# Order of work in a dense step: first normalised tile turned first, q and logits copied first, q's low part subtracted first

## The reference

```python
x = x + xattn(layernorm(x), ctx, Wq, Wkv_expand, Wout)   # 16 heads of 32, 64 keys, causal mask
x = x + ffn(layernorm(x), ...)
# xattn: q = xn @ Wq.T; scores = q k / sqrt(32); softmax; out = attn v; out @ Wout.T
# ffn:   logits = xn @ router_w.T; top 2 of 8 experts by logit, the logit is the weight;
#        y = silu(xn @ wg) * (xn @ wu) @ wd for each chosen expert, plus a shared expert with biases
```

## Time and profile before

| | before |
|---|---|
| median of 3 runs | 870.39 us (866.59 to 870.81) |
| the profiled execution | 872.62 us, of which the span is 870.9 us |
| busy in the span: TensorE matmul, VectorE | 791.0 us (91%), 614.5 us (71%) |
| ScalarE, GpSimd | 439.7 us (50%), 429.2 us (49%) |
| mean granted TensorE clock | 0.979 of full |

### The profile page before, as it was taken

The page is one execution under the profiler, slowest core; times in us unless marked ns, Lnnn a source line. Parts: engine busy times, 40 slices in busy tenths (PEclk is TensorE's granted clock), DMA queues, the critical chain, the costliest instruction groups (busy, mean ns, idle before and its releaser), DMA issues.

```text
span 870.9 us, 22280 instructions
## 1 busy us (share of the span) xinstructions
PE 791.0 (91%) x7516; PEld 545.4 (63%) x7516; DVE 614.5 (71%) x1196; ACT 439.7 (50%) x805; POOL 429.2 (49%) x530
## 2 busy tenths in 40 slices
PE   4478988989898989898999999999999999999994
PEld 1367776777777768687787787545555455455552
DVE  4978886989898989886557877555555555555552
ACT  3375766777777777777533553333333333333331
POOL 1144856565656656654600001255555555656553
PEclk9789998999999999999999999999999999999998
DMA  9324272635353534334575666488989889988892
GB/s 316 107 73 144 98 218 96 203 118 201 101 211 112 193 118 127 111 108 134 189 249 183 196 197 204 105 142 147 157 145 154 147 142 160 145 146 148 144 149 42
DMA packets 102760, 132.39 MB, mean 152 GB/s; under 512 B 54368, under 2 KB 55392, under 8 KB 101280
## 3 DMA queue, kind: packets, MB, share of 16 engines
q1 hardware_dynamic: 86784, 95.74, 37.3%
q0 software_dynamic: 15904, 35.70, 24.2%
HBM read 71.61 MB, written 52.31 MB: 142 GB/s over the span
## 4 chain that ended last, share of the span: by engine, by line
PE 46%; DVE 6%; ACT 4%; DMA 4%; issue 3%; POOL 3%; POOLq 0%; another core or an unknown queue 0%; ACTq 0%; DVEq 0%; SPq 0%
PE psum L1264 34%; PE psum L1312 8%; PE psum L1255 4%; DMA hidT<-xn2T_f 3%; DVE head_max L995 1%; DVE xy L1005 1%; DVE stats L926 1%; ACT probsT L700 1%; POOL rstd L532 1%; POOL kv_store L568 1%; ACT xn2T L700 1%; DVE w_q L1244 0%; PE psum L1364 0%; DVE hid L1219 0%; ACT attnT L700 0%
## 5 line engine op out<-in xcount | busy, mean ns | idle before, releaser
L680 POOL DMA_INDIRECT out<-w_q,tabs x71 | 112.5, 1584 | 109.1 <-DVE w_q L1244 72.9
L670 POOL DMA_INDIRECT x_in<-normed_tokens,tabs x71 | 71.0, 1000 | 137.6 <-DVE tabs L1130 88.2
L1229 DVE SCALAR_TENSOR_TENSOR hid<-psum,tabs,silu_g 128x256 f32<-128x256 f32 x71 | 34.4, 484 | 110.3 <-ACT silu_g L824 110.3
L1264 PE MATMUL psum<-exp_all,hidT 128*128 x426 | 103.4, 379 | 4.7 <-DMA hidT<-xn2T_f 4.7
L824 ACT ACTIVATE silu_g<-psum,tabs 128x256 f32<-128x256 f32 x71 | 33.7, 474 | 145.0 <-PE psum L1264 134.8
L1312 PE MATMUL psum<-xn1T,w_q 128*128 128x128 f16 x1536 | 93.3, 222 | 6.7 <-DVE xn1T L862 6.7
L1264 PE MATMUL psum<-exp_all,probsT 128*128 x420 | 96.4, 379 | 0.0
L1312 PEld LDWEIGHTS psum<-xn1T,w_q 128*128 128x128 f16 x1536 | 88.5, 99 | 7.1 <-DVE xn1T L862 6.9
L1264 PE MATMUL psum<-w_o,attnT 128*128 128x512 f16 x384 | 88.7, 381 | 0.0
L1264 PEld LDWEIGHTS psum<-exp_all,hidT 128*128 128x128 f16 x426 | 41.7, 98 | 55.8 <-issue 7.7
L530 POOL TENSOR_SCALAR rstd<-moments 128x1 f32<-128x1 f32 x64 | 14.3, 223 | 120.2 <-DVE moments L931 112.8
(11 more groups left out here) (199 smaller groups left out, 1730.2 us busy)
## 6 DMA issues: line engine op xcount, KB each, us to landing
x_in<-x SPq DMA_DIRECT2D x64, 256.0 KB, 3.1
exp_all<-experts SPq DMA_DIRECT2D x8, 1536.0 KB, 8.5
out<-xy SPq DMA_DIRECT2D x32, 256.0 KB, 2.1
normed_tokens<-xn SPq DMA_DIRECT2D x32, 256.0 KB, 2.4
normed_turned<-xn2T SPq DMA_DIRECT2D x32, 256.0 KB, 2.0
w_q<-out SPq DMA_DIRECT2D x32, 256.0 KB, 2.9
out<-w_q SPq DMA_DIRECT2D x32, 256.0 KB, 2.6
probsT<-normed_turned SPq DMA_DIRECT2D x16, 256.0 KB, 3.4
```

The lines of the kernel that those rows point to most:

```text
L670: pool.indirect_dma_start(x_in[:, t % 4, :], None, xn_dram, bass.IndirectOffsetOnAxis(gather_at[:, t:t + 1], 0)).then_inc(gathered[t % 4], 16)
L680: pool.indirect_dma_start(out, bass.IndirectOffsetOnAxis(add_at[:, t:t + 1], 0), y[:, t % Y_RING, :], None, bounds_check=TOKENS - 1, oob_i ...
L1229: dve.scalar_tensor_tensor(hid[:, :], psum[:, GU_BANK[m % 2], I:2 * I], up_scale_at[:, tm:tm + 1], silu_g[:, :], ALU.mult, ALU.mult).then_ ...
L1264: last = pe.matmul(dst, lhsT(a, c), rhs(z, c), start=(c == 0 and a == z == 0), stop=(c == n - 1 and a == 1))
```

## The change

Three engines' queues are put in another order inside a dense step. No instruction is added or taken away, and each keeps its waits.

- ScalarE: the normalisation of t5 into `xn2` goes behind the copies of q and of the logits; the `xn1T` copy of t1 goes ahead of the `xn2T` copy of t5.
- VectorE: the expert's magnitudes go behind the joining of the statistics and the low part of q.
- TensorE: the turns of t1 (`xn1`) go ahead of the turns of t5 (`xn2`).

```diff
 # scalar step
-                if live(t5):
-                    act.wait_ge(ln_rstd[1], t5 + 1)
-                    wait(act, xn2_stored[(j + 1) % 2], 16 * (TPB // 2 * b + (j - 5) // 2))
-                    act.activation(xn2[:, (j + 1) % 2, 0:H], x1, ACT.Identity, bias=rstd[:, 1, 2:3],
-                                   scale=rstd[:, 1, 1:2]).then_inc(xn2_ready, 1)
                 if live(t2):
                     act.wait_ge(q_mm, t2 + 1)
                     copy(flat(qT[:, 0, :, :]), bank(5), Q_DOWN, qT_hi)
                 if live(t6):
                     act.wait_ge(router_mm, t6 + 1)
                     copy(logits[:, bass.ds(t6, 1), :], psum[:, 6, 0:E], sc[:, S_R:S_R + 1], logits_ready)
+                if live(t5):
+                    (the same four lines)
...
+                if live(t1):
+                    act.wait_ge(xn1T_mm, t1 + 1)
+                    copy(flat(xn1T[:, 0, :, :]), bank(7), X_UP, xn1T_hi)
                 if live(t5):
                     act.wait_ge(xn2T_mm, t5 + 1)
                     wait(act, xT_stored, 16 * t5)
                     copy(flat(xn2T[:, 0, :, :]), bank(6), X_UP, xn2T_hi)
-                if live(t1):
-                    (the same two lines)
 # vector step
-                if e is not None and j in ((1, 2, 3) if isinstance(b, int) and b == 0 else (0, 2, 3)):
-                    expert_magnitudes(e, max(0, j - 1))
                 if live(tile):
                     join_stats(0, tile)
                 if live(t2):
                     dve.wait_ge(qT_hi, t2 + 1)
                     low(flat(qT[:, 1, :, :]), bank(5), Q_DOWN, flat(qT[:, 0, :, :]), qT_ready)
+                if e is not None and j in (...):
+                    expert_magnitudes(e, max(0, j - 1))
 # tensor step
+                if live(t1):
+                    pe.wait_ge(xn1_ready, t1 + 1)
+                    wait(pe, xn1T_ready, t1)
+                    transposes(bank(7), xn1[:, :], C, xn1T_mm)
                 if live(t5):
                     pe.wait_ge(xn2_ready, t5 + 1)
                     wait(pe, logits_ready, t5)
                     transposes(bank(6), xn2[:, (j + 1) % 2, :], C, xn2T_mm)
-                if live(t1):
-                    (the same three lines)
```

More of the change, by code:

```diff
@@ L752, in step @@
                     copy(logits[:, bass.ds(t6, 1), :], psum[:, 6, 0:E], sc[:, S_R:S_R + 1], logits_ready)
+                if live(t5):
+                    act.wait_ge(ln_rstd[1], t5 + 1)
+                    wait(act, xn2_stored[(j + 1) % 2], 16 * (TPB // 2 * b + (j - 5) // 2))
+                    act.activation(xn2[:, (j + 1) % 2, 0:H], x1, ACT.Identity, bias=rstd[:, 1, 2:3],
+                                   scale=rstd[:, 1, 1:2]).then_inc(xn2_ready, 1)
                 if live(t4):
@@ L763, in step @@
                     copy(flat(xn2T[:, 0, :, :]), bank(6), X_UP, xn2T_hi)
-                if live(t1):
-                    act.wait_ge(xn1T_mm, t1 + 1)
-                    copy(flat(xn1T[:, 0, :, :]), bank(7), X_UP, xn1T_hi)
                 if live(t5):
@@ L976, in step @@
                     low(flat(qT[:, 1, :, :]), bank(5), Q_DOWN, flat(qT[:, 0, :, :]), qT_ready)
+                if e is not None and j in ((1, 2, 3) if isinstance(b, int) and b == 0 else (0, 2, 3)):
+                    expert_magnitudes(e, max(0, j - 1))
                 if live(t4):
@@ L1347, in step @@
                     transposes(bank(6), xn2[:, (j + 1) % 2, :], C, xn2T_mm)
-                if live(t1):
-                    pe.wait_ge(xn1_ready, t1 + 1)
-                    wait(pe, xn1T_ready, t1)
-                    transposes(bank(7), xn1[:, :], C, xn1T_mm)
                 entry_amid(tile, entry)
```

## The result

The changed kernel takes 858.6 us (median of 4 runs, 855.61 to 863.27), the kernel before beside it 870.6 us (4 runs). The ratio is 0.987, with an interval of 0.983 to 0.991. The profiled execution took 858.63 us (before 872.62), of which the span is 856.9 us, at a mean granted clock of 0.978 (before 0.979). The forecast was 857.3 us, in a range from 850.5 to 866.5.

What follows compares the result with a forecast made beforehand. VectorE through j = 0 and 1, and the path over GpSimd and ScalarE to xn2, bound the lap. Gains 1.2 + 9.2 + 0.9 + 0.5 + 2.2 less 0.9 make 13.1 us: 857.3 us, range 850.5 to 866.5.

Steps and rivals of the forecast that it cites:

- The lap: One batch of four dense steps falls from 44.69 to 42.86 us; 1.83 us gained in each of five laps.
- the signs named: Expected in the profile: 42.9 us laps, VectorE's q wait at most 0.4, TensorE waits 0.9 and 1.4, clock 1.00 from step 11.
- TensorE's part: At j = 2, four xn1 turns run inside the wait for xn2, 0.45 us; next q 1.29 us earlier altogether.
- only ScalarE's part counts: Rival, chance 0.17: magnitudes uncovered or their DRAM way sets j = 0; a lap gains 0.63 to 0.85; 864.7 us.
- VectorE's part: Magnitudes directly ahead of attnT are covered by TensorE's scores, cost 0; without cover 1.12 us per step.
- Steps 5 to 10: Steps 6 and 7 gain nothing net; step 8 gains 0.6 and step 10 0.63, together 1.2 us.
- Steps 10 to 30: Five laps at 1.83 us give 9.2; fewer clock falls at steps 26 and 10 give 2.2, between 0 and 4.3.
- Steps 31 and 32: The two steps after the five laps gain 0.5 and 0.4 us, 0.9 together.
- Ramp: At step 2 q's low part comes up to 1.1 us earlier, then ScalarE's weight copies rule; 0.5 us gained.
- Drain: From step 34 xn2 stands behind the logits copy, which waits for the router product; 0.9 us lost, 2.2 at worst.
- only starts earlier: The experts' half behind step 37, TensorE at 9 tenths or more, gains nothing further of its own.
- The clock as a risk: Slower rival, chance 0.05: TensorE's two waits per lap each bring a 1.66 us clock fall; twelve give 879.4 us.

Runs made afterwards that it cites:

- scalar_only: Kernel before with only ScalarE's part: xn2's normalisation behind the copies of q and logits; 862.6 us, ratio 0.9886.
- vector_only: Kernel before with only VectorE's part: magnitudes behind the statistics join and q's low part; 885.29 us, ratio 1.0153.
- no_vector: Changed kernel without VectorE's part, the magnitudes where they were before; 857.36 us, ratio 0.9824 against the kernel before.
- after_again: The changed kernel measured and profiled once more, nothing altered; 858.5 us, ratio 0.9872 against the kernel before.
- mixed: Changed kernel, but magnitudes ahead of q's low part at j = 2 and 3, behind it only at j = 0; 858.8 us, ratio 0.9871.
- keys_split: Changed kernel, but at j = 1 GpSimd makes two of its four key copies behind the second normalisation's scale; 857.44 us, ratio 0.9855.
- base_late: Changed kernel, but GpSimd adds the residual's bias one step later, behind the first normalisation's scale; 867.29 us, ratio 0.9992.
- all_three: Changed kernel with magnitudes ahead of q's low part at j = 2 and 3, key copies split and bias addition late; 856.32 us, ratio 0.9861.
- load_first: all_three with SyncE's load of the next expert at j = 0 put ahead of the store of the base; 844.38 us, ratio 0.9719.

## Why the prediction was right

**The lap** is where most of the gain was to come from, and it came from there: 42.88 us by q's starts, against 42.86 predicted. The terms were 10.35 where 10.12 stood, 9.89 for 10.07, 11.48 for 11.48 and 11.15 for 11.19. So the terms read as an engine without idle time, or a path through GpSimd, were right to 0.04. The other two were off by 0.2 each way and cancelled in the sum, so that it meets the measured lap to 0.02 us is in part luck. At j = 2 to 3 the next q starts 5.11 us behind attnT's low part (229.41 - 224.30; 4.94 in the sum), and attnT's low part 5.24 behind that (5.18). The step from 3 to 0, set at TensorE's own work, is VectorE's, 9.89. Of the signs named, one failed: VectorE waits 0.46 us for q's high part at j = 3, where no wait over 0.4 us was to be left. Its wait of 1.03 us at attnT (j = 2) is for ScalarE's copy behind `xn2`, with the magnitudes done before it. The two new waits of TensorE came where they were expected and at about their size: 1.67 us at j = 1 (1.4 said), 0.97 us at j = 2 (0.9 said).

**The shares of the parts.** The sum credited TensorE's part with the 0.45 us of four turns, done inside the wait at j = 2. It is worth 0.55 a lap on top of the others and 0.7 alone. That only ScalarE's part counts is refuted: its lap alone is 43.6 against 42.88, and scalar_only is at 0.9886 [0.9861, 0.9911] of before, the change without VectorE's part at 0.9824 [0.9795, 0.9853] beside it.

**VectorE's part** was set at cost 0 for its cover and credited with freeing j = 3 and 0. The total was right, the reason was not. The cover isn't TensorE's scores but the early q: vector_only has the same scores and pays 1.07, 0.59 and 0.6 to 0.9 us in the three steps. With q early it costs 0.39 at j = 2 to 3 and saves the wait for the DRAM way at j = 0, and no_vector, at 857.36, can't be told from the full change. The conditional price that the prediction named ("without cover it is 1.12 per step") came at j = 1 to 2 alone; the other two steps paid less.

**The other terms**, from the low parts of attnT in the two profiles (after minus before): +3.13 us at step 5, +1.84 at step 10, -11.58 at step 30, -12.81 at step 32, -13.13 at step 34.

- Steps 5 to 10: 1.29 gained; 1.2 predicted.
- Steps 10 to 30: 13.42 gained; 9.2 and 2.2 for the clock predicted. Five laps of 1.82 are 9.1, so the clock gave 4.3, the upper bound of its term: both falls of before are absent in this execution. In the second profile of the changed kernel (after_again) the fall at step 10 is there, the stretch gains 11.64 and the clock 2.5, near the 2.2 of the sum. So this term differs between executions of the same kernel, and the upper bound in the first was luck.
- Steps 31 and 32: 1.23 gained, 0.9 predicted.
- Ramp: 0.5 predicted as a gain; the profile shows 3.1 later. The second profile of the same kernel is 2.9 earlier than the first. Chance of the execution, so the term was neither confirmed nor refuted.
- Drain: q of the shared entry behind it is 12.08 earlier, so 1.05 was given back from step 34 on; 0.9 predicted.
- Behind step 37 a further 1.9 us was gained, to 13.99 in all, where "only starts earlier" had stood. The second profile has no such gain: the same q is 13.30 earlier (416.21 against 429.51 us) and the execution 13.35 (859.27). So the 1.9 us are of that one execution and "only starts earlier" holds in the other.

The terms that missed (clock +2.1, behind the drain +1.9, ramp -3.6) nearly cancelled in the first profile, which is luck. In the second the ramp, taken at step 5, is 0.4 later in place of 0.5 earlier, and the clock and the end come as summed. In the medians the change is 12.0 us against 13.1.

**The clock as a risk.** Twelve waits of two kinds brought no fall in the first profile, one of 2.56 us at step 10 did in the second, and none of the 0.97 to 1.67 us that the laps have did in either. But the reason given for it, that waits of like length had brought few before, was too simple, as the last section shows.

**What was late next** was named only for TensorE. Mixed, keys_split and base_late each removed one wait and found the gain taken back within one or two steps, by a weight piece that waits for GpSimd, by the scale for the other tile, or by a store behind a load. In all three the theory named first had expected a gain; in mixed and keys_split the rival beside it came out.

## What to carry to other kernels

In an engine's queue, whatever waits longest should stand behind what is ready already; its price is not its own work but that of everything queued behind it, on this engine and on the ones that wait for it. Whether work may be moved behind a wait depends on when that wait ends: the same three lines of VectorE cost 1.5% alone and nothing with ScalarE's part. When a wait is removed and the lap doesn't shorten, look for the next queue that the moved work stands in, the DMA queue too: here an exchange of two steps on SyncE turned 856 into 844 us.

## What the runs showed of the hardware

**A wait of TensorE doesn't bring a fall of the clock by its length alone.** From step 11 on, with the granted clock going to the lower level of 1.2 GHz (the step where it falls is 1.7 us longer before and in all_three, and 1.07 in vector_only, between low parts of attnT): before, one of five waits of 2.17 us; vector_only, three of five waits of 2.15 us; all_three, one wait of 2.10 us. No wait under 2.1 us brought one there. But base_late has four waits of 3.09 to 3.39 us without any in its profile. And at step 10 of keys_split the clock fell behind waits of only 1.21 us and, at 136.72 us, 0.51 us:

```profile
135.55 0.66 PE L1260 MATMUL psum<-ident,xn 128*128 128x128 f32 x4 [1.21 <-ACT xn L756]
```

```profile
136.00:140.00 4.00, 3.49 (x20) 2.27 (x19) 2.64 (x5) 2.41 (x5) 3.61 (x5) 0.67 0.25 97
```

The turns behind the wait in vector_only, with no fall and with one:

```profile
234.37 1.06 PE L1255 MATMUL psum<-ident,xn 128*128 128x128 f32 x8 [2.15 <-ACT logits L700]
...
281.44 1.62 PE L1255 MATMUL psum<-ident,xn 128*128 128x128 f32 x8 [2.15 <-ACT logits L700]
```

and the stretch with the fall, its clock being the third number from the end:

```profile
280.00:284.00 4.00, 2.56 (x14) 2.22 (x15) 2.83 (x4) 4.00 (x9) 3.21 (x5) 0.72 0.36 132
```

What decides it, the runs don't show.

**A VectorE operation on 256 integers took 1.05 us beside a GpSimd addition and 0.17 us without it**, and all_three and load_first, which keep the addition late, show the same 0.17, but for the last expert (1.17 and 1.16 us), where an addition runs beside it again. Where VectorE is the bound, 0.88 us of it was 0.88 us of the step.
